# Two of the norms between the stages of a transformer kernel, moved into the stages beside them

## The reference

```python
x = L0_attn_x
x = _layernorm(x + _L0_attn_ref(x, ...))   # linear attention
x = _layernorm(x + _L0_ffn_ref(x, ...))    # 8 experts, two per token, and a shared one
x = _layernorm(x + _L1_attn_ref(x, ...))   # attention with softmax features, causal
x = _layernorm(x + _L1_ffn_ref(x, ...))    # six layers of local attention and a gated network
```

## Time and profile before

| | us |
|---|---|
| three runs | 4785.08, 4775.87, 4784.36 |
| their median | 4784.36 |
| the profiled execution: time | 4782.15 |
| the profiled execution: span in the profile | 4780.4 |
| expert stage, loop of eight iterations | 190.2 to 468.1 |
| norm `_n1` | 469.2 to 490.2 |
| feature stage | 491.9 to 1283.3 |
| norm `_n2` | 1283.7 to 1305.0 |
| deep stage | 1305.3 to 4780.4 |

### The profile page before, as it was taken

How to read it: one execution, slowest core, us unless ns; L and a number is a source line. 1 busy time by engine, 2 the same in 40 slices (tenths; PEclk the granted TensorE clock), 3 DMA queues, 4 the chain that set the end, 5 groups by cost and what they waited for, 6 DMA issues and landing times.

```text
span 4780.4 us, 164817 instructions
## 1 busy us (share of the span) xinstructions
PE 4240.7 (89%) x70208; PEld 3352.6 (70%) x70208; DVE 4081.5 (85%) x6282; ACT 3053.0 (64%) x5515; POOL 3026.4 (63%) x1586
## 2 busy tenths in 40 slices
PE   5698699999668999999999999999989999999996
PEld 4565377877656777777777777777767777777775
DVE  4344699999789998999999999899999999999995
ACT  3365333333156777777777777777777777777773
POOL 0222566666267777677777777767677677777762
PEclk9699799999889999999999999999999999999998
DMA  1234000000023233332333323332242332423232
GB/s 50 78 127 141 0 1 0 0 0 0 19 61 70 61 74 88 72 74 62 75 86 74 75 64 90 74 77 66 65 100 62 75 69 65 96 67 78 64 67 66
DMA packets 237661, 302.78 MB, mean 63 GB/s; under 512 B 92500, under 2 KB 127832, under 8 KB 236504
## 3 DMA queue, kind: packets, MB, share of 16 engines
q1 hardware_dynamic: 221752, 247.08, 22.6%
q0 software_dynamic: 15264, 46.14, 3.1%
HBM read 50.37 MB, written 28.84 MB: 17 GB/s over the span
## 4 chain that ended last, share of the span: by engine, by line
DVE 41%; PE 15%; issue 8%; POOL 5%; ACT 3%; DMA 0%; POOLq 0%; DVEq 0%; SPq 0%
DVE raw L1906 10%; DVE raw L1913 8%; DVE mx L1964 3%; DVE ss L1900 3%; DVE E L1970 3%; PE shared L1565 3%; PE acc L1672 2%; DVE den L1977 2%; POOL spare L2129 2%; PE sco L1640 2%; POOL raw L2137 2%; DVE hT L2027 2%; PE shared L1567 2%; PE shared L1566 2%; ACT raw L1783 1%
## 5 line engine op out<-in xcount | busy, mean ns | idle before, releaser
L2137 POOL TENSOR_TENSOR raw<-raw,rs 128x1024 f32<-128x1024 f32 x384 | 793.4, 2067 | 885.5 <-DVE rs L1934 549.3
L2129 POOL TENSOR_TENSOR spare<-raw,table 128x1024 f32<-128x1024 f32 x384 | 971.9, 2541 | 62.8 <-DVE raw L1913 47.1
L1913 DVE TENSOR_TENSOR raw<-raw,spare 128x1024 f32<-128x1024 f32 x384 | 736.5, 1918 | 13.2
L1906 DVE TENSOR_TENSOR raw<-raw,table 128x1024 f32<-128x1024 f32 x384 | 668.2, 1740 | 89.3 <-POOL spare L2129 87.6
L1783 ACT ACTIVATE raw<-shared 128x512 f32<-128x512 f32 x768 | 463.4, 603 | 297.7 <-PE shared L1567 268.4
L1565 PE MATMUL shared<-wqkv_lo,xT_hi 128*128 128x512 f32 x1152 | 550.2, 478 | 57.6 <-DVE xT_lo L1943 48.1
L2154 POOL TENSOR_TENSOR E<-E,rden 128x512 f32<-128x512 f32 x384 | 553.7, 1462 | 30.6 <-DVE rden L1979 30.5
L1900 DVE TENSOR_REDUCE ss<-spare 128x16 f32<-128x1024 f32 x384 | 463.6, 1207 | 46.9 <-ACT spare L1788 46.4
L1620 PE MATMUL trn<-ident,raw 128*128 128x128 f32 x3072 | 484.4, 280 | 7.6 <-POOL raw L2137 4.0
L1566 PE MATMUL shared<-wqkv_hi,xT_lo 128*128 128x512 f32 x1152 | 462.9, 402 | 0.1
L1788 ACT ACTIVATE spare<-shared 128x512 f32<-128x512 f32 x768 | 461.5, 601 | 1.9 <-DVE ss L1900 1.9
(11 more groups left out here) (208 smaller groups left out, 9734.1 us busy)
## 6 DMA issues: line engine op xcount, KB each, us to landing
Vw<-V SPq DMA_DIRECT2D x1344, 128.0 KB
xs<-X SPq DMA_DIRECT2D x144, 128.0 KB, 2.1
Vw<-V SPq DMA_DIRECT2D x192, 64.0 KB
e_plain<-in_L_ffn_W SPq DMA_DIRECT2D x16, 704.0 KB, 4.7
split_hi<-e_high POOLq DMA_DIRECT2D x16, 704.0 KB, 5.9
split_lo<-e_low POOLq DMA_DIRECT2D x16, 704.0 KB, 7.1
wqkv_hi<-split_hi POOLq DMA_DIRECT2D x30, 256.0 KB, 3.1
wqkv_lo<-split_lo POOLq DMA_DIRECT2D x30, 256.0 KB, 3.2
```

The lines of the kernel that those rows point to most:

```text
L1906: dve.tensor_tensor(x, x, table[:, part, 0, k][:, None, :].to_broadcast([P, H, HD]), ALU.mult).then_inc(cos_part, 1)
L1913: dve.tensor_tensor(x, x, t2[:, part], ALU.add).then_inc(summed, 1)
L2129: pool.tensor_tensor(dst, src, by[:, None].to_broadcast([P, H, 2, 32]), ALU.mult).then_inc(sin_part, 1)
L2137: pool.tensor_tensor(x, x, rs[:, at:at + H][:, :, None].to_broadcast([P, H, HD]), ALU.mult).then_inc(rotated, 1)
```

## The change

**In the expert stage** the norm `_n1` is done block by block. VectorE takes the statistics of a block one step after its add (s = 14, 23, 32 and, for the last block of an iteration, s = 40 behind its add), POOL raises them to the power -1/2, one column at a time, between its low halves, and VectorE norms the block some steps later (s = 6 of the next iteration, s = 22, and two at s = 39). The loops of VectorE and POOL are written out; those of TensorE and ScalarE are kept.

**At the beginning of the deep stage** the norm `_n2` is done in five parts, of 4, 4, 8, 8 and 8 blocks. Part 0 stands before `body`; the statistics of parts 1 to 4 stand at the steps 3, 9, 16 and 23 of `Pair(0, -1)`, POOL's powers at the same steps, the products four steps later. `bring` waits for the part in which its sequence lies. The copy of `X` to DRAM moves into the first `body` on SP, behind a staging and a wait for all five parts; VectorE waits for it before its first addition to `X` and no longer before the first `body`. The four table loads stand before the first staging.

```diff
@@ expert_stage, POOL @@
             with pool.Fori(0, NI) as i:
                 stage(i)
-            stage(NI)
-            for j in range(2):
-                low_unit(0, j)
-            with pool.Fori(1, NI - 1) as i:
+            def power(b):
+                pool.wait_ge(n_kept, count(b + 1))
+                pool.tensor_tensor(n_rstd[:, b:b + 1], n_ve[:, b:b + 1], n_half[:], ALU.pow).then_inc(n_powered, 1)
+
+            pool.wait_ge(n_half_set, count(1))
+            for i in range(NI - 1):
                 stage(NI + i)
-                for j in range(2):
-                    low_unit(i, j)
+                if i > 0:
+                    power(4 * i - 1)
+                low_unit(i, 0)
+                power(4 * i)
+                low_unit(i, 1)
+                power(4 * i + 1)
+                power(4 * i + 2)
             stage(2 * NI - 1)
+            power(4 * NI - 5)
...
-            for j in range(2):
-                low_unit(NI - 1, j)
+            low_unit(NI - 1, 0)
+            power(4 * NI - 4)
+            low_unit(NI - 1, 1)
+            for b in range(4 * NI - 3, 4 * NI):
+                power(b)
@@ expert_stage, VectorE @@
-            with dve.Fori(0, NI) as i:
+            dve.memset(n_half[:], -0.5).then_inc(n_half_set, 1)
+
+            def statistics(b):
+                dve.wait_ge(added, count(b + 1))
+                dve.bn_stats(n_st[:, b % 2], X[:, b]).then_inc(n_stats, 1)
+                dve.wait_ge(n_stats, count(b + 1))
+                dve.bn_aggr(n_mv[:, b], n_st[:, b % 2]).then_inc(n_means, 1)
+                dve.wait_ge(n_means, count(b + 1))
+                dve.tensor_scalar(n_ve[:, b:b + 1], n_mv[:, b, 1:2], EPS_LN, None, ALU.add).then_inc(n_kept, 1)
+
+            def normal(b):
+                dve.wait_ge(n_powered, count(b + 1))
+                dve.tensor_scalar(X[:, b], X[:, b], n_mv[:, b, 0:1], n_rstd[:, b:b + 1],
+                                  ALU.subtract, ALU.mult).then_inc(n_applied, 1)
+
+            for i in range(NI):
...
+                    if s >= 14 and (s - 14) % (NE + 1) == 0 and s < UN:
+                        statistics(4 * i + (s - 14) // (NE + 1))
+                    if s == UN + 4:
+                        statistics(4 * i + 3)
+                    if s == 6 and i > 0:
+                        normal(4 * i - 1)
+                    if s == 22:
+                        normal(4 * i)
+                    if s == UN + 3:
+                        normal(4 * i + 1)
+                        normal(4 * i + 2)
+            normal(4 * NI - 1)
@@ deep_stage @@
+FIRST_PARTS = ((0, 4), (4, 8), (8, 16), (16, 24), (24, 32))
+FIRST_STEPS = (3, 9, 16, 23)
...
@@ SP @@
             sp.dma_start(mask32, c["mask"][:, 0:P]).then_inc(const_in, 16)
-            sp.dma_start(kept, X[:].rearrange("p b d -> p (b d)")).then_inc(x_kept, 16)
...
+                if q.n + d < NSEQ:
+                    sp.wait_ge(first_normed, count(first_part(q.n + d) + 1))
                 sp.dma_start(xs[:], X[:, bass.ds(2 * q.place(d), 2), :]).then_inc(staged, 16)
...
                 if q.has(3):
                     bring(q, 3)
+                if q.n == 0:
+                    sp.wait_ge(first_normed, count(len(FIRST_PARTS)))
+                    sp.dma_start(kept, X[:].rearrange("p b d -> p (b d)")).then_inc(x_kept, 16)
...
+            for j in range(4):
+                load_table(0, j)
             bring(Pair(0, 0), 0)
             bring(Pair(0, 0), 1)
-            for j in range(4):
-                load_table(0, j)
@@ VectorE @@
+                if q.n + d == 0:
+                    dve.wait_ge(x_kept, 16)
...
+            def first_statistics(i):
+                lo, hi = FIRST_PARTS[i]
+                for b in range(lo, hi):
+                    t = dve.bn_stats(last_st[:, b], X[:, b])
+                t.then_inc(first_stats, 1)
+                dve.wait_ge(first_stats, count(i + 1))
+                for b in range(lo, hi):
+                    t = dve.bn_aggr(last_mv[:, b], last_st[:, b])
+                t.then_inc(first_means, 1)
+                dve.wait_ge(first_means, count(i + 1))
+                dve.tensor_scalar(last_ve[:, lo:hi], last_mv[:, lo:hi, 1], EPS_LN, None, ALU.add).then_inc(first_kept, 1)
...
+            def first_of(q, at):
+                if q.n == -2 and at in FIRST_STEPS:
+                    first_statistics(1 + FIRST_STEPS.index(at))
+                if q.n == -2 and at - 4 in FIRST_STEPS:
+                    first_normal(1 + FIRST_STEPS.index(at - 4))
...
                     if q.has_block():
                         feed(q, at)
+                    first_of(q, at)
                     last_of(q, at)
...
             dve.memset(half, -0.5).then_inc(filled, 1)
+            first_statistics(0)
...
+            first_normal(0)
             dve.wait_ge(const_in, 16)
...
-            dve.wait_ge(x_kept, 16)
@@ POOL @@
+            def first_powers(i):
+                lo, hi = FIRST_PARTS[i]
+                pool.wait_ge(first_kept, count(i + 1))
+                pool.tensor_tensor(last_rstd[:, lo:hi], last_ve[:, lo:hi],
+                                   half[:, 0:1].to_broadcast([P, hi - lo]), ALU.pow).then_inc(first_powered, 1)
...
+            pool.wait_ge(filled, count(1))
+            first_powers(0)
             load_w1(0)
@@ network @@
-            norm_stage(nc, X, "_n1")
             feature_stage(nc, X, c, feature)
-        norm_stage(nc, X, "_n2")
```

27 lines of the change are left out of this document (added).

## The result

The changed kernel takes 4755.68 us, the median of 5 runs (4752.34 to 4762.93), against 4784.36 for the kernel before (5 runs beside them, 4775.87 to 4785.08): a ratio of 0.9947, 95% interval 0.9936 to 0.9958, so 28.7 us less. The forecast was 4748 with a range of 4736 to 4764. The direction and the range hold; the forecast difference was 36.5 us, so by the medians some 8 of them did not come. The prediction was worked out from one profiled execution.

The account below looks back on a forecast made before the run. Both norms were taken to bound the kernel, as only VectorE and POOL work in them while TensorE idles. Terms -20.0, 0, -21.6, -1.8 and +6.9 gave -36.5 us, hence 4748 us, 8 in 10 within 4736 to 4764.

Parts of the forecast that it names:

- The tail and what was removed: End of expert stage: 23.8 us between last add and feature copy go; block 31's statistics, power and product leave 1.66.
- The boundary, 2.1 taken between 1.70 and 2.44: Change from expert to feature stage: 2.1 us from the norm's end to the feature copy.
- The rival on the boundary: End of expert stage: the last low half's DMA holds the stage, at most 1 us; no chance given.
- The expert loop at 0: Expert loop: the first norm's statistics, powers and products are hidden, 0 us added, bounds 0 and 30.
- The deep stage begins 21.6 earlier: Second norm: the deep stage's first instruction follows the feature stage's end by 0.35 us, 21.6 us less.
- The first staging, -1.8: Deep stage's start: staging does not wait for the norm; first transpose 9.1 us in against 10.9, 1.8 us less.
- The ramp, +6.9 with bounds of 4.8 and 17: Deep stage, sequences 0 and 1: parts 1 to 4 of the second norm add 6.9 us of 17 us work.
- The sum: Whole kernel: -20.0 + 0 - 21.6 - 1.8 + 6.9 = -36.5 us.
- Full clock at the start of the feature stage: Rival, chance 0.10: after only about 4.7 us idle TensorE begins the feature stage at full clock, 8 us less, 4740.
- POOL did not make TensorE wait inside the loop: Rival, chance 0.03: POOL's copies in the expert loop come late behind powers and delay TensorE; 4804 at 8 us late.
- Part of it stays visible: Rival, chance 0.12: 10 us or more of the moved work in expert loop and ramp stays visible, 4758 to 4772.
- Its own signs: Profile after: right if feature copy near 472; wrong if last expert add 5 us later or ramp products three times as long.

Follow-up runs that it names:

- drain_early: The change with the powers' constant set first in the expert stage and an extra POOL drain before the last block's power; 4749.23 us, ratio 0.9930 to the kernel before.
- on_scalar: drain_early with the second norm's 28 products of parts 1 to 4 moved from VectorE to ScalarE; 4742.22 us, ratio 0.9914 to the kernel before.

## Why the prediction was right, and where it was not

- **The tail and what was removed.** Right: the 23.8 us are gone, the tail of block 31 took 1.73 against 1.66.
- **The boundary, 2.1 taken between 1.70 and 2.44.** Wrong: 4.16. The bounds were taken from stages whose last engine was VectorE. The change makes POOL the last but one, and with it POOL's closing drain of 3.45 us comes onto the path; with the drain paid earlier (drain_early) the exit is 3.9, where the forecast's own terms give 4.05. The rival on the boundary named the last low half's DMA and gave it 1 us at most; the wait was there, on the same engine, but it is the drain, and it was in the trace of before: the first norm began 1.10 us after the last add where the second began 0.36 after the stage ahead of it, which was read as the cost of leaving the stage. The rows of the barrier's line, with POOL's drain ending at 468.9, had not been read.
- **The expert loop at 0.** Right for the loop, 264.3 against 263.9, and by its reason: the limit of lateness was tried with two and four times the statistics. Left out was the way into it. The prediction checked what is queued behind POOL's powers but not behind POOL's first wait of all, for the constant: 2 to 3 us.
- **The deep stage begins 21.6 earlier.** Right: the norm's stage is gone, and the first instruction follows the feature stage's end by 0.35 us as forecast. The table has 20.1 because the feature stage took 1.5 longer in this execution.
- **The first staging, -1.8.** It came to -1.2: first transpose 9.75 us in, where 9.1 was forecast and 10.9 stood before (low half of x 11.2 in, against 12.5). The staging did wait for the norm, since VectorE's means stood 1.59 us for SP to raise the counters. The prediction counted SP's increments for SP's own DMAs and not for those who wait on a counter.
- **The ramp, +6.9 with bounds of 4.8 and 17.** It was 13.0: between the low half and the end of the second inverse norm there were 51.8 us before and are 64.7 now. By the steps: part 1 was put at 0 and cost 2.5. Part 2 was put at 4.8; 6.7 us to the first inverse norm less part 1's 2.5 leave 4.2. Parts 3 and 4 were put at 2.1 and cost 6.3. The step that failed is that products beside POOL were priced at their own length or hidden: they took 4.22 for 1.11, 5.84 and 4.19 for 2.12. Told by kind it is plainer. Of the forecast's 6.9 the products had 2.7 (2.2 in part 2, 0.5 in part 4) and the statistics 4.2 (2.6, 1.4, 0.2). The run on_scalar, which moved the products and added only the short operations, took 8.5 off and left 4.5 for all the rest. So the statistics were priced well and the products at a third of their cost. The epsilon of part 4, 8 columns that take 0.17 elsewhere, took 2.11, beside POOL as well:

```profile
1331.19 4.66 POOL L2227 TENSOR_TENSOR spare<-raw,table 128x1024 f32<-128x1024 f32 x2
```

```profile
1331.46 2.11 DVE L2115 TENSOR_SCALAR last_ve<-last_mv 128x8 f32<-128x8 f32 x1
```

The rule of the Trainium skill that was weighed against the rows (GPSIMD Engine Reference, section 8, with VectorE: DVE Perf Modes, Mode 2×_2P) says that this contention exists for single-source fp32 work in SBUF, and it was right where the prediction had found no row to decide it. Applied to part 4 alone it made 1 us; it should have been applied to every product that stands beside POOL. By the same pages a `tensor_reduce`, which has one source and no two-port mode (The perf-mode tier table), is free of it, and here the trace agrees: the sum of squares at 1289.52 took its usual 1.22 beside POOL. So did the statistics at 1312.39, 1.64 for eight blocks beside POOL's scaling.
- **The deep stage in all.** +11.7 at the second inverse norm and +8.4 at the end. The 3 us between them need not have been regained: over the seven profiled executions with the changed deep stage its mean is 3483.6, over the two with the old one 3472.1, and the difference, 11.5, is that of the ramp. With two executions and a scatter of several us this is a hint and no proof.
- **The sum.** -36.5, and +2.1 for the drain, +2.2 for the entry, +0.4 for the loop, +3.3 for the deep stage (8.4 in place of 5.1) and +1.5 of the feature stage are -27.0; with the 3.4 of the start that is the -23.6 between the spans. That the time fell within the range is in part luck: the drain and the entry lay outside every bound that the sum had for them (4.16 against at most 2.44, and 2.2 against 0), and the range held them only because it had been drawn towards the ramp's upper bound of 17, of which the ramp took 13.
- **The rivals.** Full clock at the start of the feature stage did not come: TensorE stood idle for 6.8 us (480.52) and still had the half clock, granted 0.50 in the first 20 us of the stage, as before. Nor did it come at the rival's own condition of 4.7 us: in drain_early TensorE stood idle for 4.50 us and was granted 0.50 for the 20 us from its first work on. POOL did not make TensorE wait inside the loop. "Part of it stays visible" asked for 10 us or more; 6.1 us more came in the ramp and none in the loop.
- **Its own signs.** Of what the profile after was to show when the prediction was wrong, two things came: the last add 6 us later, though not by the loop's doing, and products in the ramp at almost four times their length (4.22 for 1.11). Of the signs that it was right, the feature copy came at 479.98 in place of 472 and the first inverse norm 6.7 us later, not 5, counted from the low half of x.

## What to carry to other kernels

Before an engine is given the last work of a stage, look at its row in the closing barrier: a drain that used to lie beside other work comes onto the path, and it can be paid earlier, in that engine's last wait. A new wait is checked from the first instruction that stands behind it in its queue, the one-time waits for constants included. When element-wise work is added to a busy stretch, ask what the neighbour engine does at that moment: four products of VectorE took 4.22 us beside POOL and 1.12 two steps earlier, and ScalarE took 1.65 for them, for the most part beside POOL.

## What the runs showed that was not expected

- POOL's first drain in the expert stage takes 3.4 to 4.8 us in the kernels with the first norm in it (2.9 to 4.3 behind the operation ahead of it) and 6.3 in the kernel before, where it begins while the last DMA is being issued; where it begins within 1.3 us of that issue it ends 5.6 us after it; a second one in the same stage takes 0.63 to 0.83, with 0.54 of a power in it. In the feature stage the first one takes 0.1 behind its operation.
- A product of VectorE of 334 ns, started beside an operation of POOL, took up to 2435 ns. ScalarE's version came every 0.4 us with and without POOL beside it.
- More code of VectorE ahead of a stage went with lost time in that stage's loop: 9.5 us of idle time without a releaser, 1.8 to 2.1 us at each of five jumps back, in two kernels that differ from a third by instructions in another stage alone.
- TensorE had the half clock (granted 0.50) at the feature stage's start after 4.50 us without work as after 24.8.
